# A graph network of four layers on one core: edges placed by one-hot products with bit keys instead of scatters, src and dst gathered in the edge loop, weight folds double-buffered

## The reference

```python
row, col = (edge_index[0], edge_index[1])          # src, dst
edge_feature = jax.nn.silu(edge_rbf @ We1 + be1) @ We2 + be2
msg = edge_feature * x[col]
agg = jax.ops.segment_sum(msg, row, num_segments=N_NODES)
return x + (jax.nn.silu(agg @ Wn1 + bn1) @ Wn2 + bn2)
```

## Time and profile before

| | |
|---|---|
| median of 3 runs | 1371.45 us (1371.29 to 1372.97) |
| the profiled execution | 1371.52 us |
| its span | 1369.7 us |
| TensorE busy | 1193.7 us, 87% |
| VectorE busy | 850.1 us, 62% |
| ScalarE busy | 676.4 us, 49% |
| POOL busy | 612.5 us, 45% |
| mean granted clock of TensorE | 0.94 of full speed |

### The profile page before, as it was taken

One profiled execution on the slowest core, in us unless ns is written; L12 is line 12 of the kernel. 1 busy time (PEld: TensorE's weight loads), 2 busy tenths in 40 slices (PEclk: granted clock), 3 DMA queues, 4 the chain that ended last, 5 costly groups with the idle time before them and its releaser, 6 DMA issues.

```text
span 1369.7 us, 21273 instructions
## 1 busy us (share of the span) xinstructions
PE 1193.7 (87%) x6133; PEld 994.5 (73%) x6133; DVE 850.1 (62%) x1489; ACT 676.4 (49%) x1300; POOL 612.5 (45%) x679
## 2 busy tenths in 40 slices
PE   1488307999999999999999999999887999897867
PEld 1355206888888888888888888887867788786666
DVE  6455205777777777777777777777556343273662
ACT  2467404666666666666666666665531232222231
POOL 5888766555555555555455555552502020131110
PEclk9699657999999999999999999999998999999978
DMA  8455112222222222222222222221100101010101
GB/s 245 147 185 186 33 12 66 77 77 77 77 77 77 77 77 77 75 77 76 67 82 73 74 75 71 75 77 51 39 1 32 62 31 61 32 62 31 39 1 38
DMA packets 31131, 98.20 MB, mean 72 GB/s; under 512 B 10125, under 2 KB 10375, under 8 KB 26746
## 3 DMA queue, kind: packets, MB, share of 16 engines
q0 software_dynamic: 22592, 56.08, 14.4%
q1 hardware_dynamic: 8506, 41.67, 8.8%
HBM read 88.18 MB, written 9.42 MB: 71 GB/s over the span
## 4 chain that ended last, share of the span: by engine, by line
PE 75%; POOL 10%; DVE 7%; issue 4%; ACT 2%; DMA 1%; DVEq 0%; SPq 0%; ACTq 0%; POOLq 0%
PE ps L785 11%; PE ps L787 11%; PE ps L786 11%; POOL slots_dram L443 10%; PE ps L778 8%; PE ps L779 8%; PE ps L780 8%; PE ps L876 3%; PE ps L875 3%; PE ps L880 3%; PE ps L792 3%; PE ps L793 3%; PE ps L997 1%; PE ps L841 1%; DVE zb_lo L1461 1%
## 5 line engine op out<-in xcount | busy, mean ns | idle before, releaser
L785 PE MATMUL ps<-we_hi,s_hi 128*128 128x512 f32 x680 | 274.1, 403 | 0.0
L786 PE MATMUL ps<-we_lo,s_hi 128*128 128x512 f32 x680 | 266.5, 392 | 0.0
L787 PE MATMUL ps<-we_hi,s_lo 128*128 128x512 f32 x680 | 266.5, 392 | 0.0
L468 POOL DMA_INDIRECT xg<-h_dram,node_picks x170 | 173.0, 1018 | 98.6 <-POOL node_picks L458 67.1
L462 POOL DMA_INDIRECT rbf<-in_edge,edge_picks x170 | 189.4, 1114 | 51.7 <-issue 50.0
L615 ACT ACTIVATE m_hi<-msg 128x512 fp32r<-128x512 f32 x170 | 107.3, 631 | 166.1 <-DVE msg L1308 165.9
L1313 DVE TENSOR_TENSOR m_lo<-msg,m_hi 128x512 fp32r<-128x512 f32 x170 | 117.7, 692 | 91.0 <-ACT m_hi L615 91.0
L443 POOL DMA_INDIRECT slots_dram<-fields,row_i x111 | 141.0, 1270 | 48.0 <-issue 48.0
L541 POOL TENSOR_TENSOR w_lo<-wstage,w_hi 128x2048 fp32r<-128x2048 f32 x9 | 41.8, 4639 | 252.0 <-ACT w_hi L707 252.0
L605 ACT ACTIVATE s<-ps,be 128x256 f32<-128x256 f32 x340 | 133.9, 476 | 36.7 <-PE ps L780 36.7
L787 PEld LDWEIGHTS ps<-we_hi,s_lo 128*128 128x128 f32 x680 | 128.0, 188 | 28.2
(11 more groups left out here) (245 smaller groups left out, 2645.4 us busy)
## 6 DMA issues: line engine op xcount, KB each, us to landing
stage<-in_fold_a SPq DMA_DIRECT2D x6, 1024.0 KB, 5.6
stage<-in_fold_b SPq DMA_DIRECT2D x6, 1024.0 KB, 8.4
fold_dram<-folded SPq DMA_DIRECT2D x6, 1024.0 KB, 4.0
wstage<-fold_dram SPq DMA_DIRECT2D x6, 1024.0 KB, 4.7
w_raw<-in_nodew SPq DMA_DIRECT2D x3, 1024.0 KB, 17.4
wstage<-in_selfw SPq DMA_DIRECT2D x3, 1024.0 KB, 6.1
rbf<-in_edge,edge_picks POOLq DMA_INDIRECT x170, 2.8
xg<-h_dram,node_picks POOLq DMA_INDIRECT x170, 3.4
```

Of the source, the lines that this page charges most:

```text
L468: pool.indirect_dma_start(xg[t.slot][:, j], None, h_dram, bass.IndirectOffsetOnAxis(ap=node_picks[t.slot][:, j:j + 1], axis=0)).then_inc(x ...
L785: pe.matmul(outp, lh, rh, start=False, stop=False, skip_group_check=True)
L786: pe.matmul(outp, lh, rl, start=False, stop=False, skip_group_check=True)
L787: return pe.matmul(outp, ll, rh, start=False, stop=False, skip_group_check=True)
```

## The change

The scatters, `slots_dram`, `table`, `srccol` and `dstcol` are gone. All 165 columns are placed by products, in 28 groups of up to six columns. For a group VectorE makes `hot_lo` and `hot_hi` for six columns with one instruction each, on 16-bit operands laid out in pairs of columns; ScalarE multiplies `hot_lo` by a key (`mark`), whose bits, partition number and group number, sit in a 16-bit float; TensorE makes one product of 128x170 for each column (`place`), each of the six into a PSUM region of its own, of which there are six. At the end VectorE adds the regions up: the sum's bits give partition and group, the region in which it lies the column within the group, all three together the number of the edge (`slot_row`). Which groups follow which quarter of which fold stands in the table `AFTER`.

src and dst are written once to `ends_dram`, 8 bytes an edge. In each step of the loop POOL gathers them for 256 edges with two indirect transfers more (`end_ids`), behind the two for the edge rows and as far ahead; `node_picks` is copied from `end_ids`, with a wait for it and a counted semaphore (`nodes_known`) ahead; VectorE has one small instruction more (`edge_ends`), which subtracts the bucket's base. The one-hots are made from its result `ends`.

The folds have two buffers each for `stage`, the split parts and `folded` (the second ones lie where the node weights come later). Fold 0 multiplies its factors unsplit in fp32: 16 products instead of 48. The factors of a fold are split quarter by quarter beside the products of the fold ahead. norm, edge weights and bucket tables stand at fixed places among the folds. Since the second buffers occupy their place, the node weights are loaded after fold 5, and they are split in the last three steps of the edge loop. POOL's constants are made in another order.

The core of the diff:

```diff
+GROUP = 6
+GROUPS = (ET + GROUP - 1) // GROUP
+HOT_RING = 3
+AFTER = (((), (0,), (1, 2), (3, 4)), ((5, 6), (7,), (8, 9), (10,)), ((11, 12), (13,), (14, 15), (16,)),
+         ((17, 18), (19,), (20, 21), (22,)), ((23, 24), (25,), (26, 27), ()), ((), (), (), ()))
+REGION = 256
+KEY_ONE, KEY_SHIFT, KEY_P = 127 << 10, 13, 7
...
+            load_factors(0)
+            load_factors(1)
             sp.dma_start(x_res[:], a["x"].rearrange("(c p) f -> p c f", p=NC)).then_inc(x_in, 16)
-
+            sp.wait_ge(ends_packed, 4)
+            sp.dma_start(ends_dram[0:1], no_end[:]).then_inc(ends_saved, 16)
+            sp.dma_start(ends_dram[1:].rearrange("(p t) w -> p (t w)", p=EP),
+                         end_rows[:].rearrange("p t w -> p (t w)")).then_inc(ends_saved, 16)
+            sp.wait_ge(fold_mm, K)
+            load_factors(2)
+            save_product(0)
...
+            for m in range(3, FOLDS):
+                sp.wait_ge(split_lo, K * (m - 2))
+                load_factors(m)
+                save_product(m - 2)
...
             def pick_edges(t):
 
                 t.wait(pool, rT_mm, 1, -1)
-                pool.tensor_copy(edge_picks[t.slot][:], table[:, bass.ds(t.count(2), 2), 0]).then_inc(picked, 1)
+                t.wait(pool, ends_ready, 1, -1)
+                pool.tensor_copy(edge_picks[t.slot][:], slot_row[:, bass.ds(t.count(2), 2)]).then_inc(picked, 1)
 
             def pick_nodes(t):
                 t.wait(pool, msg_ready, 2, -2)
-                pool.tensor_copy(node_picks[t.slot][:], table[:, bass.ds(t.count(2), 2), 2]).then_inc(picked, 1)
+                pool.wait_ge(ends_in[t.slot], t.rounds(32))
+                pool.sem_inc(nodes_known, 1)
+                pool.tensor_copy(node_picks[t.slot][:], end_ids[t.slot][:, :, 1]).then_inc(picked, 1)
 
             def gather_edges(t):
                 for j in range(2):
                     pool.indirect_dma_start(
                         rbf[t.slot][:, j], None, a["edge"],
-                        bass.IndirectOffsetOnAxis(ap=edge_picks[t.slot][:, j:j + 1], axis=0)).then_inc(rbf_in[t.slot], 16)
+                        bass.IndirectOffsetOnAxis(ap=edge_picks[t.slot][:, j, 0:1], axis=0)).then_inc(rbf_in[t.slot], 16)
+                for j in range(2):
+                    pool.indirect_dma_start(
+                        end_ids[t.slot][:, j], None, ends_dram,
+                        bass.IndirectOffsetOnAxis(ap=edge_picks[t.slot][:, j, 1:2], axis=0)).then_inc(ends_in[t.slot], 16)
...
+            for m in range(FOLDS):
                 for u in range(K):
...
+                    for i in AFTER[m][u]:
+                        mark(i)
+                    if m + 1 < FOLDS:
+                        factor_high(m + 1, u)
+                    if (m, u) == (2, 1):
+                        norm(0)
+                    if (m, u) == (3, 1):
+                        weights_high(0, 2)
+                    product_out(m, u)
...
+            def place(i):
+
+                pe.wait_ge(hots_hi_made, i + 1)
+                pe.wait_ge(marks_made, i + 1)
+                r = i % HOT_RING
+                for j in range(min(GROUP, ET - i * GROUP)):
+                    mm = pe.matmul(ps[:, 5 + j // 2, j % 2 * REGION:j % 2 * REGION + TILES],
+                                   marked[r][:, j // 2, :, j % 2], hot_hi[r][:, j // 2, :, j % 2],
+                                   start=False, stop=False, skip_group_check=True)
+                mm.then_inc(perm_mm, 1)
...
+            def edge_ends(t):
+
+                s = t.slot
+                dve.wait_ge(ends_in[s], t.rounds(32))
+                t.wait(dve, hots_ready, 3, -3)
+                dve.tensor_tensor(ends[s][:], end_ids[s][:], base2[:, bass.ds(t.count(2), 2)],
+                                  op=ALU.subtract).then_inc(ends_ready, 1)
...
                 message_lo(t, 0)
                 message(t, 1)
+                if t.reg is None and t.c >= STEPS - 3:
+                    weights_low(t.c - STEPS + 5, t.c - STEPS + 6)
```

More of the change, by code:

```diff
@@ L200, in build @@
         loop = Region(main.at)
[L201 removed]
+        edge_picks = [loop(f"edge_picks{i}", [P, 2, 2], I32) for i in range(2)]
         node_picks = [loop(f"node_picks{i}", [P, 2], I32) for i in range(2)]
         rbf = [loop(f"rbf{i}", [P, 2, R], F32) for i in range(2)]
+        end_ids = [loop(f"end_ids{i}", [P, 2, 2], I32) for i in range(2)]
+        ends = [loop(f"ends{i}", [P, 2, 2], F32) for i in range(2)]
         xg = [loop(f"xg{i}", [P, 2, F], F32) for i in range(2)]
@@ L248, in build @@
[L248 to L257, removed]
@@ L837, in turn_rows @@
+            pe.wait_ge(perm_zeroed, 1)
+            for m in range(FOLDS):
+                for u in range(K):
+                    fold(m, u)
+                    for i in AFTER[m][u]:
+                        place(i)
             def turn_rows(t):
@@ new lines, in hots @@
+            def hots(i):
+                r = i % HOT_RING
+                if i >= HOT_RING:
+                    dve.wait_ge(perm_mm, i - HOT_RING + 1)
+                else:
+                    dve.wait_ge(pos_ready, 2)
+                    dve.wait_ge(ends_packed, 4)
+                for at, hot, iota, w, made in ((lo16, hot_lo, iota_lo, P, hots_lo_made),
+                                               (hi16, hot_hi, iota_hi, TILES, hots_hi_made)):
+                    pair = at[:, i * GROUP:i * GROUP + GROUP].rearrange("p (j u) -> p j u", u=2)
+                    dve.tensor_tensor(hot[r][:], iota[:, None].to_broadcast([EP, GROUP // 2, w, 2]),
+                                      pair[:, :, None].to_broadcast([EP, GROUP // 2, w, 2]),
+                                      op=ALU.is_equal).then_inc(made, 1)
@@ L1261, in _ @@
-            each(dve, FOLDS, fold)
-            link(dve.tensor_scalar(bucket_f[0][:], step_row[:], first[0:1, 1:2], None, ALU.is_ge))
-            for b in range(2, C):
-                o = bucket_f[(b + 1) % 2] if b < C - 1 else bucket_row
-                link(dve.scalar_tensor_tensor(out=o[:], in0=step_row[:], scalar=first[0:1, b:b + 1],
-                                              in1=bucket_f[b % 2][:], op0=ALU.is_ge, op1=ALU.add))
-            dve.wait_ge(perm_mm, PERM)
-            perm3 = ps[:, 5, 0:3 * TILES].rearrange("p (b t) -> p b t", b=3)
@@ new lines, in _ @@
+            for m in range(FOLDS):
+                for u in range(K):
+                    for i in AFTER[m][u]:
+                        hots(i)
+                    if m + 1 < FOLDS:
+                        factor_low(m + 1, u)
+                    if (m, u) == (1, 3):
+                        dve.wait_ge(x_in, 16)
+                        for c in range(C):
+                            row_stats(c)
+                    if (m, u) == (2, 1):
+                        norm(0)
+                    if (m, u) == (3, 1):
+                        weights_low(0, 2)
+                    if (m, u) == (4, 1):
+                        bucket_tables()
@@ L1292, in rows_lo @@
+            for part in range(2):
+                dve.tensor_scalar(slot_row[:, :, part], number[2][:], float(part - GROUP * (KEY_ONE >> KEY_P)), 0.0,
+                                  ALU.add, ALU.max).then_inc(table_ready, 1)
+            dve.wait_ge(consts_ready, 17)
             def rows_lo(t):
```

453 lines of the change are left out of this document (219 added, 234 removed).

## The result

The changed kernel takes 1440.26 us (median of 4 runs, 1432.43 to 1449.96) against 1371.74 us; the ratio is 1.050, 95% interval 1.0435 to 1.0568. It is 5% slower. The forecast was 1353 us, and its range ended at 1400.

A forecast was written before the change was run, and what follows sets the result against it. POOL's scatters were taken to bound the front and TensorE the loop, with POOL becoming the loop's limit after the change. 1371.5 - 81 (front) + 52 (loop) + 10 (end) = 1352.5, forecast 1353 us, range 1312 to 1400.

The forecast's parts named there:

- The front, -81: Before the edge loop: without scatters, TensorE starts on the edges at 130 us instead of 211, saving 81 us.
- third rival: Folds in front: one-hots run at one element a cycle, the front gives only 64 us, total 1370 us; chance 0.08.
- The end, +10: Last three loop steps: node-weight splits on ScalarE and VectorE delay message_lo, costing 10 us, bounds 4 and 14.
- POOL's own step, 9.3: Edge loop: with two id gathers and a counted semaphore, POOL needs 9.3 us a step, bounds 8.8 and 10.0.
- The distrust of the quiet price: Edge loop: gathers cost 1.06 us, not the quiet 0.94, because VectorE's two-input work (s_lo, m_lo) meets them.
- first rival: Edge loop: POOL stays hidden, with a step of 8.8 us or less, total 1301 to 1312 us; chance 0.12.
- The step is POOL's own work: Edge loop: POOL at 9.3 us a step, against TensorE's 8.67, sets the pace, costing 52 us over 82 steps.
- a gather's price doesn't follow its bytes: Edge loop, pricing the id gathers: 128 rows of 512 B take 1114 ns, of 2 KB 1018 ns; 1.06 us taken.
- second rival: Edge loop: POOL's step eats the gain through its in-order queue; at 9.8 us a step 1393 us; chance 0.20.
- The last doubt of the forecast: Edge loop: the forecast is wrong if TensorE's granted clock, 0.99, falls with the short idle times.

The follow-up runs named there:

- 64-byte run: The changed kernel with each id gather fetching 64 bytes per id row instead of 8, the surplus unread: 1315.9 us, ratio 0.9607 to before.
- memset run: The kernel before with two memsets of 1400 floats on POOL added to each step, no transfer added: 1481.3 us, ratio 1.0807.
- 32-byte run: The changed kernel with each id gather fetching 32 bytes per id row instead of 8: 1381.7 us, ratio 1.008 to before.
- run 256: No separate run: 256 is the packet size in bytes of the 32-byte run (changed kernel, 32 bytes fetched per id row, 1381.7 us).
- short memsets: The kernel before with two memsets of 650 floats on POOL added to each step, no transfer added: 1370.83 us, ratio 0.9989.

## Why the prediction was wrong, step by step

- **The front, -81: right.** TensorE starts on the edges at 126.5 (forecast 130), the first edge gather is issued at 120.3 (forecast 125), the first node gather is 81.4 us earlier. The one-hots take 0.55 and 0.68 us (0.46 and 0.59), a mark 0.94 (0.8), a split 1.04 and 1.23 (0.97 and 1.15), each a little more, and the table is ready 5 us earlier all the same. The third rival, one element a cycle, fell: 0.68 us for 1020 elements, where VectorE's 32-bit operation of 1024 takes 1.23. By "VectorE: DVE Perf Modes" of the Trainium skill (The perf-mode tier table) 16 bits give twice the rate; the trace agrees.
- **The end, +10: right** (+10.8; 11.7 to 13 where the loop is even).
- **POOL's own step, 9.3: too high.** It is 8.82 where nothing is waited for, my lower bound, in after and, over the whole stretch, with 64-byte rows. The two added gathers took 0.97 us each in the mean (0.94 with 64-byte rows) and not 1.06. The counted semaphore cost nothing: with 64-byte rows the copies stand 0.13 us apart (602.50, 602.63), the pitch of the earlier trace rows. (In after they stand 0.53 apart, because edge_picks took 0.57.) The distrust of the quiet price was right for other gathers. In the 64-byte run, from 300 to 800 us, those that met VectorE's s_lo took 1.17 us in the mean, all others 0.95; in after it was 1.02 and 0.97. "GPSIMD Engine Reference" (Specifications) of the Trainium skill says that POOL shares SBUF interfaces with VectorE, with contention where VectorE has two SBUF inputs; the trace agrees for s_lo. It agrees only in part for m_lo, which has two inputs too: gathers that met m_lo and not s_lo took 1.06 us in before and 0.945 in the 64-byte run. With 8.8 the sum is 1312 us, the first rival's upper end, and the runs with 64 bytes and more give 1316.
- **"The step is POOL's own work": the step that failed.** It is the sentence "POOL becomes the limit". The memset run shows what that would look like. Even at 8.8 it was not so for sure: without id gathers POOL waits 1.9 us a step for VectorE and the step is 8.82 all the same, so that is TensorE's own pace now. In after no engine is the limit (POOL 536 of 906 us, VectorE 565, TensorE 797 with the clock lowered in part), and 1.5 us a step come from a cost of the id gathers that lies on no engine's time. I wrote that a gather's price doesn't follow its bytes. For POOL that is true from 8 bytes to 2 KB. For the others it isn't below 64 bytes: in place of a full POOL the runs show TensorE's counts coming late while small rows are gathered, which costs 124 us (1440.26 against 1315.9) and is gone with rows of 64 bytes. The nearest rows, the scatters of 16 bytes, gave no warning: 111 of them ran from 23 to 197 us, one in 1.6 us, mostly beside TensorE's folds, and no wait of that stretch is on "remote". They read SBUF and write DRAM, the gathers go the other way. A range that only looked at POOL's time ended too low.
- **The second rival** came out nearer in time (1393) by the wrong mechanism. The last doubt of the forecast, that TensorE's clock could fall with short idle times, was right: the products of after took 45 us longer than those of the run without id gathers, at a clock of 0.93 against 0.98.

## To carry to other kernels

Price an added small transfer not only by the time of its issue: where many small rows are gathered and POOL is nearly full, give each gathered row 64 bytes or more, even if the surplus is thrown away, before blaming the queue. When a loop gets uneven and no engine is full, look for waits on "remote" and compare the size of the transfers first. To tell a full queue from what it carries, fill it with another size of the same thing, and measure the filler's own time before trusting it.

## What was not expected of the hardware

- Undisturbed gathers of 128 rows took POOL 0.94 to 0.95 us with 8, 64, 512 or 2048 bytes a row, and 0.86 with 16 rows of 8 bytes.
- Two gathers a step with rows of 8 bytes made the mean step 1.1 to 1.5 us longer, in both kernels; with 64 bytes nothing. In those runs TensorE's counts come late, up to 8 us behind its records and several within 0.3 us. Why small rows do that stayed open: whether it is the read or the write of under 64 bytes no run here tells. Every execution that was timed was also recorded (each has a span and a granted clock), and in these loops some count events are missing from the trace (from 300 to 800 us after has 35 of turn_rows' counts for 48 steps, before 58 for 58). So no run tells either whether the recording has a part in it. "DMA: Bandwidth & Descriptors" of the Trainium skill (Specifications) names 512 bytes as the size below which a transfer is done as read-modify-write and loses bandwidth. These runs show their limit between 32 and 64 bytes a row: 64 bytes did no harm that 512 didn't do. But the trace packs the rows of a 128-row gather by eight: the packets of the 64-byte run have 512 bytes, those of the 32-byte run 256. So the table can't tell 64 bytes of a row from 512 of a packet. The size of a packet alone isn't it, for the gathers of 16 rows had packets of 8 bytes and no wait on "remote".
- TensorE idle for 1.1 us a step, evenly, as in the run with long memsets (443 of 500 us busy), kept the granted clock at 0.99; the 3.91 us at once in after were followed by 6.2 us at 0.50.
- The loop without id gathers is still 12 us longer than before (8.82 us a step for 8.68) although TensorE is not idle in it from 300 to 800 us. It is in TensorE's own pace: the 24 products of second_layer stand 233 to 235 ns apart in the median where they stood 227 to 230 before, which makes some 0.1 to 0.14 us a step. The runs with one gather, with 16-row gathers and with 64-byte rows have the same pace, those with short memsets and with two added wide gathers the old one. Why is not explained.
